# Eight transformer stages on one core: the last stage's job bank is emptied by one copy, its turned batches move to another bank, and the first norm waits for one batch

## The reference, cut to what matters

```python
q_in  = layernorm(x)            # 8 x 512 x 256
kv_in = layernorm(context)      # the same norm weights
q = q_in @ wq + bq              # 256 -> 16 heads of 64
k, v = split(kv_in @ wkv + bkv)
scores = (q . k) / 8            # per head, 512 x 512, causal
x = x + concat(softmax(scores) @ v) @ wo + bo
```

## Time and profile before

| | us |
|---|---|
| median of 3 runs | 4040.84 (4038.7 to 4043.15) |
| the profiled execution's own time | 4025.74 |
| its span, first to last instruction | 4024.0 |
| TensorE busy | 3666.0, 91% of the span |
| DVE, ACT, POOL busy | 2789.9, 2471.4, 1992.5 |
| mean granted TensorE clock | 0.966 of full speed |

### The profile page before, as it was taken

One profiled execution on the slowest core, in us unless ns is written; L12 is line 12 of the kernel. 1 busy time (PEld: TensorE's weight loads), 2 busy tenths in 40 slices (PEclk: granted clock), 3 DMA queues, 4 the chain that ended last, 5 costly groups with the idle time before them and its releaser, 6 DMA issues. The chain is left out here.

```text
span 4024.0 us, 68608 instructions
## 1 busy us (share of the span) xinstructions
PE 3666.0 (91%) x21586; PEld 2034.7 (51%) x21586; DVE 2789.9 (69%) x6843; ACT 2471.4 (61%) x5253; POOL 1992.5 (50%) x1987
## 2 busy tenths in 40 slices
PE   5999999997978999999999999997898898888998
PEld 2444444444863344433333344445776666666665
DVE  3666677774656777799998877765765655566554
ACT  2555577775324777788888777773346665655564
POOL 3555523332322233378888633313436666666665
PEclk9999999998988999999998899998999999999999
DMA  4433344331003533332222343421000000000000
GB/s 102 103 81 83 80 109 87 84 84 33 1 11 67 121 87 82 77 85 64 59 65 60 70 108 84 89 65 39 11 11 6 12 7 12 6 12 8 11 7 6
DMA packets 135373, 220.51 MB, mean 55 GB/s; under 512 B 42720, under 2 KB 44640, under 8 KB 133216
## 3 DMA queue, kind: packets, MB, share of 16 engines
q1 hardware_dynamic: 135008, 216.02, 23.2%
HBM read 59.69 MB, written 5.51 MB: 16 GB/s over the span
## 5 line engine op out<-in xcount | busy, mean ns | idle before, releaser
L1099 ACT ACTIVATE prob<-ST 128x512 f32<-128x512 f32 (+3 forms) x2304 | 1151.3, 567 | 433.9 <-PE ST L646 430.1
L1317 DVE TENSOR_REDUCE mx<-MX 128x1 f32<-128x512 f32 x1536 | 963.1, 682 | 218.0 <-PE MX L646 216.9
L646 PE MATMUL MX<-stk 48*128 48x512 f32 (+3 forms) x2560 | 893.1, 439 | 58.9 <-DVE mx L1310 14.5
L646 PE MATMUL ST<-stk 50*128 50x512 f32 (+3 forms) x2560 | 914.2, 441 | 3.2 <-ACT prob L1099 1.8
L646 PEld LDWEIGHTS MX<-stk 48*128 48x128 f32 x2560 | 417.9, 190 | 703.6 <-DVE mx L1317 296.9
L1762 POOL TENSOR_SCALAR prob<-prob,mx 128x128 f32<-128x128 f32 (+3 forms) x512 | 560.3, 1108 | 370.1 <-DVE mx L1497 369.8
L646 PE MATMUL OUT<-prob,V 128*32 128x512 f32 (+3 forms) x5120 | 661.1, 589 | 8.0 <-POOL prob L1704 4.6
L646 PEld LDWEIGHTS ST<-stk 50*128 50x128 f32 x2560 | 421.2, 188 | 54.0 <-ACT prob L1099 25.8
L1310 DVE CUSTOM_DVE_ANT_0 MX<-MX,W_even 128x512 f32<-128x512 f32 x512 | 347.2, 700 | 36.9 <-PE MX L646 36.4
L1697 POOL TENSOR_TENSOR prob<-prob,W_odd 128x512 f32<-128x512 f32 x256 | 324.5, 1283 | 87.3 <-ACT prob L1099 86.9
L1314 DVE CUSTOM_DVE_ANT_0 MX<-MX,later 128x128 f32<-128x128 f32 (+3 forms) x512 | 237.6, 518 | 120.1 <-PE MX L646 119.4
(11 more groups left out here) (186 smaller groups left out, 7293.6 us busy)
## 6 DMA issues: line engine op xcount, KB each, us to landing
stk<-hi SPq DMA_DIRECT2D x640, 128.0 KB, 3.8
stk<-lo SPq DMA_DIRECT2D x320, 128.0 KB, 3.9
misc<-misc SPq DMA_DIRECT2D x160, 128.0 KB, 2.6
sums<-spread SPq DMA_DIRECT2D x80, 256.0 KB
misc<-in_ctx_t SPq DMA_DIRECT2D x24, 512.0 KB, 6.9
W_even<-in_w SPq DMA_DIRECT2D x2, 2048.0 KB, 10.5
XH<-in_ctx_rows SPq DMA_DIRECT2D x8, 512.0 KB, 3.5
X<-in_x_t SPq DMA_DIRECT2D x1, 3584.0 KB, 14.1
```

The lines of the kernel that those rows point to most:

```text
L646: return nc.tensor.matmul(o, l, r, start=start, stop=stop)
L1099: nc.scalar.activation(prob_at(k)[:, q0:S], STB[k % RING][:, q0:S], ACT.Copy if addmask else ACT.Exp).then_inc(ex_done, 2 if addmask else 1)
L1317: nc.vector.tensor_reduce(m, bank[:, :], AX.X, ALU.max).then_inc(mx_red, 1)
```

## The change

In the last stage: (a) keys and queries leave the job bank by one activation, in full; the high part is a copy of it from SBUF to SBUF, made by ACT one step later (`high_queries_keys`), with a semaphore of its own, on which DVE's low part waits, itself one step later than before. (b) The turned batches go into `OUT3`, the value products' bank, and are emptied by one activation too; their high parts follow in steps 5 and 6 (`high_source`), their low parts in steps 6 and 7. TensorE waits for the emptied product before the first of them, for the first before the second, and for the second before the value product of step 6. The count of jobs in `JOB3` no longer has them. (c) DVE adds an output to X before it empties the transposed tiles of the same step, and not after. At the start: (d) the first batch of X has a semaphore of its own, on which DVE and POOL wait; for the others DVE waits before the statistics of the second batch. (e) ACT makes an activation of one column as soon as the constants are there.

```diff
-            sp.dma_start(X[:, 0:NT, :], x_in[:, 0:NT, :]).then_inc(x_loaded, 16)
+            sp.dma_start(X[:, 0:NT, :], x_in[:, 0:NT, :]).then_inc(x_first, 16)
...
@@ TensorE, layer3
                     wait(pe, at3_done, Q)
+                    if u.turn and pair == 0:
+                        pe.wait_ge(turn3_free, turn3(u, 1) + 1)
...
-                def turn_batch(u, name, c, N):
+                def turn_batch(u, c, N):
                     if c == 0:
                         pe.wait_ge(xh_ready, N + 1)
-                    free_bank(job3(u, name, c))
-                    turn_tiles(c, JOB3).then_inc(job3_full, 1)
+                        pe.wait_ge(at3_done, 2 * u.v)
+                    else:
+                        pe.wait_ge(turn3_free, turn3(u, c))
+                    turn_tiles(c, OUT3).then_inc(turn3_full, 1)
@@ ScalarE, layer3
                     for t in range(STEPS3):
+                        if u.more and 1 <= t < 5:
+                            high_queries_keys(u, t - 1)
+                        if u.turn and t in (5, 6):
+                            high_source(u, t - 5)
                         if u.on:
                             exp_tiles(u, t)
...
-                    to, full = (x[:, (u.r + 1) % 2, n // 2, kind, :] for x in (QK[0], QK_full))
-                    nc.scalar.activation(to, bank[:, :], ACT.Identity, **how)
-                    nc.scalar.activation(full, bank[:, :], ACT.Identity, **how).then_inc(job3_free, 1)
+                    nc.scalar.activation(QK_full[:, (u.r + 1) % 2, n // 2, kind, :], bank[:, :], ACT.Identity, **how
+                                         ).then_inc(job3_free, 1)
+
+                def high_queries_keys(u, n):
+                    act.wait_ge(job3_free, job3(u, "kq", n) + 1)
+                    to, full = (x[:, (u.r + 1) % 2, n // 2, n % 2, :] for x in (QK[0], QK_full))
+                    nc.scalar.activation(to, full, ACT.Copy).then_inc(qk3_high, 1)
+
+                def high_source(u, c):
+                    act.wait_ge(turn3_free, turn3(u, c) + 1)
+                    to, full = source3(u)
+                    nc.scalar.activation(to[0][:, c, :], full[:, c, :], ACT.Copy).then_inc(src3_high, 1)
...
-                def turned(u, name, c, even):
-                    act.wait_ge(job3_full, job3(u, name, c) + 1)
-                    to, full = (cT3[even], cT3_full[even]) if name == "tc" else (hT3, hT3_full)
-                    turned_to(to, full, c, JOB3).then_inc(job3_free, 1)
+                def turned(u, c):
+                    act.wait_ge(turn3_full, turn3(u, c) + 1)
+                    _, full = source3(u)
+                    nc.scalar.activation(full[:, c, :], OUT3[:, :], ACT.Identity, **scale_shift(s, c)).then_inc(turn3_free, 1)
...
+            act.wait_ge(consts_in, 48)
+            nc.scalar.activation(warm[:, :], cols[:, 0:1], ACT.Identity).then_inc(warmed, 1)
             act.wait_ge(pool_ready, 1)
@@ VectorE, attention
+                            if r == 0 and (s, u) == (SELF0, -1):
+                                dve.wait_ge(x_loaded, 16)
@@ VectorE, layer3
+                        if (u.bs, u.r) == (0, 0) and t == 6:
+                            bias_out(u)
+                        if u.tail and t >= 6:
+                            add_out(u, t - 6)
                         if t >= 2 and u.on:
                             turned_out(u, t - 2)
                         if t < 2 and u.tail:
                             turned_out(Unit3(*u.back()), t + 6)
-                        if (u.bs, u.r) == (0, 0) and t == 6:
-                            bias_out(u)
-                        if u.tail and t >= 6:
-                            add_out(u, t - 6)
-                        if u.more and 1 <= t < 5:
-                            low_queries_keys(u, t - 1)
-                        if u.turn and t in (5, 6):
-                            dve.wait_ge(job3_free, job3(u, TURNS[u.r], t - 5) + 1)
-                            low_source(u.r - 1, (u.bs + 1) % 2, t - 5)
+                        if u.more and 2 <= t < 6:
+                            low_queries_keys(u, t - 2)
+                        if u.turn and t >= 6:
+                            dve.wait_ge(src3_high, turn3(u, t - 6) - 3)
+                            low_source(u.r - 1, (u.bs + 1) % 2, t - 6)
...
-            dve.wait_ge(x_loaded, 32)
+            dve.wait_ge(x_first, 16)
...
-            pool.wait_ge(x_loaded, 32)
+            pool.wait_ge(x_first, 16)
```

More of the change, by code:

```diff
@@ L124, in program @@
         qabs = sb("qabs", [P, 4])
+        warm = sb("warm", [P, 1])
         qst = sb("qst", [P, 16])
@@ L200, in PT3_of @@
             return PT[:, at:at + S - P * kt]
-        x_loaded, consts_in = sem("x_loaded"), sem("consts_in")
+        x_first, x_loaded, consts_in = sem("x_first"), sem("x_loaded"), sem("consts_in")
         w_in = [sem(f"w_in{s}") for s in range(8)]
@@ L211, in program @@
         shapes_done, pool_ready = sem("shapes_done"), sem("pool_ready")
-        quant = sem("quant")
+        warmed, quant = sem("warmed"), sem("quant")
         quant_pe = sem("quant_pe")
@@ L234, in program @@
         bias3, later3_set, cols3_in = sem("bias3"), sem("later3_set"), sem("cols3_in")
-        first3_full, first3_free = sem("first3_full"), sem("first3_free")
-        qk3_low, src3_low = sem("qk3_low"), sem("src3_low")
+        turn3_full, turn3_free = sem("turn3_full"), sem("turn3_free")
+        qk3_high, qk3_low = sem("qk3_high"), sem("qk3_low")
+        src3_high, src3_low = sem("src3_high"), sem("src3_low")
         job3_full, job3_free = sem("job3_full"), sem("job3_free")
@@ L399, in out_job @@
             return L_NO[(s + 1, 0, "O1") if b == NB - 1 and s + 1 in JOINED else (s, 2 * b + 2, "O1")]
-        TURNS = {1: "tc", 2: "tx"}
+        TURNS = (1, 2)
         def jobs_of(bs, r):
-            more, turn = R3 * bs + r + 1 < UNITS3, r in TURNS and 0 <= bs < NB - 1
             names = []
[L408 to L415, removed]
+            if R3 * bs + r + 1 < UNITS3:
+                names += [("kq", n) for n in range(4)] + [("v", n) for n in range(2)]
             if (bs, r) == (0, 0):
@@ L428, in job3, with source3, turn3 @@
             return JOB_NO[u.bs, u.r, (name, n)] + JOBS_OF_TWO * u.k
+        def source3(u):
+            even = (u.bs + 1) % 2
+            return (cT3[even], cT3_full[even]) if u.r == 1 else (hT3, hT3_full)
+        def turn3(u, c):
+            return 4 * (u.b + 1) + 2 * (u.r - 1) + c
         class Unit3:
@@ L599, in slot @@
                     if u.r == 0 and u.norm_next:
[L600 to L603, removed]
+                        sp.wait_ge(turn3_full, 4 * u.b + 4)
                         load_ctx_rows(u.b + 1)
@@ L859, in turn_first @@
                     pe.wait_ge(xh_ready, norm3(0, which) + 1)
-                    pe.wait_ge(*((first3_free, 2) if which else (ml_evac, 2 * NB * (m + 1))))
+                    pe.wait_ge(*((turn3_free, 2) if which else (ml_evac, 2 * NB * (m + 1))))
                     for c, bank in enumerate((LA, LB)):
-                        turn_tiles(c, bank).then_inc(first3_full, 1)
+                        turn_tiles(c, bank).then_inc(turn3_full, 1)
                 turn(0)
@@ L888, in slot @@
                         if u.turn and t in (4, 5):
-                            turn_batch(u, TURNS[u.r], t - 4, norm3(u.b + 1, u.r - 1))
+                            turn_batch(u, t - 4, norm3(u.b + 1, u.r - 1))
                         if t == 2 and u.tail:
@@ L1003, in layer3 @@
                 pe.wait_ge(w3_low, 3)
-                pe.wait_ge(first3_free, 4)
+                pe.wait_ge(turn3_free, 4)
                 run_slots3(pe, slot)
@@ L1145, in batch @@
                             for c, bank in enumerate((LA, LB)):
-                                act.wait_ge(first3_full, 2 * which + c + 1)
-                                turned_to(to, full, c, bank).then_inc(first3_free, 1)
+                                act.wait_ge(turn3_full, 2 * which + c + 1)
+                                turned_to(to, full, c, bank).then_inc(turn3_free, 1)
                 split_weights()
@@ L1170, in slot @@
                         if u.turn and t in (4, 5):
-                            turned(u, TURNS[u.r], t - 4, (u.bs + 1) % 2)
+                            turned(u, t - 4)
                         if t == 2 and u.tail:
@@ L1387, in low_first @@
                     for c in range(NC):
-                        dve.wait_ge(first3_free, 2 * which + c + 1)
+                        dve.wait_ge(turn3_free, 2 * which + c + 1)
                         low_source(which, 0, c)
@@ L1771, in norm_part @@
                     elif t == 1:
-                        turned = JOB_NO[u.bs, 1, ("tc", 1)] + JOBS_OF_TWO * u.k
-                        rows_centre(N, xt(u.b + 1, 0, NT), job3_full, turned + 1)
+                        rows_centre(N, xt(u.b + 1, 0, NT), turn3_full, 4 * (u.b + 1) + 2)
                     else:
```

4 lines of the change are left out of this document (2 added, 2 removed).

## The result

The changed kernel takes 3944.2 us (3937.08 to 3950.26), the kernel before beside it 4041.86: ratio 0.9759, interval 0.9740 to 0.9778, 97.7 us less. Two more series on other chips gave 0.9752 (0.9726 to 0.9777) and 0.9767 (0.9743 to 0.9791). The forecast was 3968 with a range down to 3952; the direction and the mechanism held, the gain was larger than the range allowed.

What follows compares the result with a forecast made beforehand. TensorE was taken to bound the kernel, standing for the shared job bank in the last stage. 63 us there plus 9.8 at the start gave 73, so 4040.84 - 73 = 3968 us, range 3955 to 3981, wider range 3952 to 3990.

Steps and rivals of the forecast that it cites:

- Step (1): Job bank, last stage: one copy out saves 0.58 at each of 32 V0, leaving 19 us; the other QK_full waits go.
- Step (2): ACT, last stage: later high-part copies of 0.62 fit into its idle time before the exponentials; priced at nothing.
- Step (3): Last stage, ahead of K0: DVE adds the output before copying the transposed tiles, so the whole 18.4 us goes.
- Step (6): Start: first norm no longer waits for all of X, 8.5 us; table load runs earlier, 1.3; together 9.8, kept throughout.
- Rivals A to D: A: POOL/DVE queues, 3985, 0.14; B: V0's wait stays, 3987, 0.05; C: other waits replace, 4031, 0.05; D: exponentials delayed, 4062, 0.04.
- the 10 to 20 forecast: Sign of being right, in the profile after: POOL's prob holds TensorE for some 10 to 20 us.
- the last stage, 79.0 for 63: Last stage: TensorE's waits for the job bank, 91.4 us, less 19, 6 and 3 us, give 63 us saved.
- Step (5), POOL at r = 1: Units with r = 1: earlier projections only meet POOL's queue; 0.9 taken off in each of 7 units, 6 us.
- Step (5), r = 2: Head of r = 2: T1's low part delays the copy freeing Q0's bank; 0.45 in 7 units, 3 us taken off.
- a surplus: Last stage: more gain than forecast, with the leftover of V0's wait partly gone too; chance 0.02.

Runs made afterwards that it cites:

- the three edits: Kernel before with one edit each: addition before copying, 4008.3 us; turned batches in OUT3, 4007.88 us; one copy of keys and queries, 4001.42 us.
- V0 apart: Changed kernel with V0 moved into OUT3 as well, so it no longer waits for ACT's copy of Q1: 3931.69 us, ratio 0.9741.
- one moved instruction: Changed kernel with V0 in OUT3, plus POOL's bias addition moved from r = 1 to r = 0 in seven batches: 3929.47 us, ratio 0.9726.
- the first and the second edit alone: Kernel before with one edit each: DVE adds the output before copying the transposed tiles, 4008.3 us; turned batches go into OUT3, 4007.88 us.

## Why the prediction fell short, step by step

**Right.** The place: one bank through which all jobs pass, and the first norm's wait. Step (1): V0 keeps 0.40 to 0.61, 18.0 us over the stage (19 forecast), and of the other waits for QK_full, 11.5, 3.6 are left where none were forecast. (V0's wait before was 0.64 to 1.42, 36.0 in all, and not 1.18 at each.) Step (2), priced at nothing: ACT still waits for DVE ahead of the exponentials. Step (3): K0 starts without a wait for X; of the 18.4, 0.9 stood ahead of the last output and stays. Step (6): 9.55 us at hT for 9.8, held next by the bias row. Rivals A to D fall by the runs above: POOL holds 12.3 us, within the 10 to 20 forecast, V0's wait halves, each edit alone pays, and ACT still stands ahead of the exponentials.

**The term that failed: the last stage, 79.0 for 63.** The step that failed is the pricing of a stand, and with it the 9 us taken off for the queues. Five pieces, from TensorE's idle time and the start-to-start times of its groups over the whole stage (second profile of before against second of after):

- The price of a stand was read as the idle time ahead of the matmul. A K0, V1 or O0 that needn't wait starts mostly 0.06 to 0.08 before the modelled end of the score ahead. Together with the groups around the turned batches, which became shorter by 0.05 to 0.16, the time outside the idle rows fell by 9.8 us. Nothing in the sum stood for it, though a K0 with no wait and one with a wait could have been laid side by side in the trace of before: at 3372.91 a K0 there starts 0.07 before the score ahead of it ends, with no idle time.
- T0's own wait, 2.0, was in none of the rows that I added up.
- Step (5), POOL at r = 1: 6 us were taken off. The tiles' turn behind K1 waits 0.89 (0.70 before) and the one behind V0 0.25 (none before): 0.44 in 7 units, 3.1 us.
- Step (5), r = 2: 3 us were taken off for the low part ahead of the first minimum. Q0's wait there went from 0.15 to 0.18: 0.2 us.
- The other way: V0, the other waits for QK_full and X gave 0.5, 0.7 and 0.3 less than was added up, 1.5 us together.

63 + 9.8 + 2.0 + 2.9 + 2.8 - 1.5 = 79.0, where this pair measured 1041.1 - 960.8 = 80.2; the idle time alone fell from 111.3 to 40.8, that is 70.5. The losses that step (5) named came to 3.3 us, and the 4 us by which the three edits fall short of their sum agree with that.

**The rest.** Stage and start come to 79.0 + 9.5 = 88.5, while the three series of the changed kernel gave 94 to 100 with intervals that begin at 84 to 90. The last 6 to 12 us are in no row. Averaged over six profiles each, what lies ahead of the last stage took 2994.4 with the old start (2984.0 to 3003.4) and 2983.8 with the new (2976.8 to 2989.6), 10.6 less, so these stages hide no large gain. Executions of one kernel lie up to 30 us apart, and in the profiles they do so in the stages that the change doesn't touch; part of the rest may be that scatter. This is argued, not shown: two of the three intervals begin 1 to 2 us above 88.5, and the rest stays open.

**The range.** Its lower end allowed 16 us more than the forecast, nearly all of it from losses that wouldn't come; a surplus got 2 in 100, for V0's leftover, and a larger gain per stand was not thought of. 4040.84 - 88.5 = 3952.3 would have been at its edge even by the rows alone.

## What to carry to other kernels

Where an engine stands at the same place many times, the idle row need not be all that its removal pays (the stage became 80.2 us shorter in one pair of profiles, its idle time by 70.5; V0 apart gave 13 for 18.0): compare a group ahead of a stand with the same group where nothing waits, and let the range reach further on the side of the gain. A bank shared by everything is the first thing to look at when the busiest engine stands a little before each of its jobs; emptying it in one copy, adding before copying and giving one class of jobs another bank were worth some 17 to 36 us each here, and next came the queue of the slowest helper in the units with extra work, which one moved instruction relieved. And compare two profiles by their stages, at like granted clock, before the difference of two executions is explained: even the last stage's own length moved by 3 to 4 us between executions of the same code (958.0 with a granted clock of 0.94 over its last 60 us and 961.0 with 0.86, but 1037.0 and 1041.2 both with 0.89).

## What was not expected of the hardware

- The granted clock of the same stretch of the same program differs between executions: over the first 100 us it was 0.98 twice, 0.88 once and 0.78 or 0.79 four times with the old start, 0.98, 0.93 and 0.88 once each and 0.77 or 0.78 four times with the new one. The first stage is about 6 us shorter at 0.98 than at 0.78, but with the same start it was shorter still at 0.88 and 0.93.
- Behind a score and without a wait, a job of the job bank (K, Q, V or O) begins mostly 0.06 to 0.08 us before the modelled end of that score (in the last stage of before, of the changed kernel, and of those with the first and the second edit alone), though it writes another bank. Where K0 stood 0.63, it began 0.06 behind the end of DVE's addition, and the stand had cost 0.63 + 0.06.
- A turned batch of four 128 x 128 transposes took 0.66 us in the job bank and 0.60 in the value products' bank, start to start 0.59 and 0.53. The bank doesn't decide it. In the 14 profiles a batch takes 0.65 or 0.66 wherever it begins 0.05 to 0.06 after DVE's copy has emptied its bank of the values, in either bank, and 0.60 wherever the bank has been free for 0.23 or more; the 15 in between take 0.63. Pairs of DVE's copy and the batch in the same bank, first before (T1), then with one copy of keys and queries alone (T0, job bank), then with V0 apart (T0, value products' bank):

```profile
3555.77 0.69 DVE L1513 COPY V<-ST 128x512 f32<-128x512 f32 x1 [1.70 <-PE ST L646]
3556.52 0.66 PE L656 MATMUL ST<-ident,XH 128*128 128x128 f32 x4
```

```profile
3538.91 0.69 DVE L1521 COPY V<-ST 128x512 f32<-128x512 f32 x1 [1.18 <-PE ST L647]
3539.84 0.60 PE L657 MATMUL ST<-ident,XH 128*128 128x128 f32 x4
```

```profile
3525.05 0.69 DVE L1546 COPY V<-L 128x512 f32<-128x512 f32 x1 [0.51 <-PE L L648]
3525.80 0.66 PE L658 MATMUL L<-ident,XH 128*128 128x128 f32 x4
```

In the first pair the batch even begins before the modelled end of the tiles' turn ahead, so that no idle row shows it, and still the two together took some 0.13 us longer than where the bank had long been free.
